# Turning the softmax weights and the inverse sums of a four-layer graph network with the DMA crossbar instead of TensorE

## The chip, the cores and the metric

The kernel runs on one core of a Trainium2 chip. The metric is the device time of one execution in microseconds (us), median of several.

## The reference, cut to what matters

Four graph-attention layers, each behind a layer norm and a relu, each added to its input. There are 32 independent items of 512 nodes with 256 features, all in float32.

```python
h = relu(layernorm(x)); x = x + L0(h)   # e = leaky(h1 @ h2.T), masked; softmax; relu(att @ h3)
h = relu(layernorm(x)); x = x + L1(h)   # 4 heads: e = leaky(e_src[i] + e_dst[j]), masked; softmax; elu(att @ q)
h = relu(layernorm(x)); x = x + L2(h)   # 4 heads of 64: softmax(Q K^T / 8, masked) @ V, @ Wo + bo, layernorm
h = relu(layernorm(x)); x = x + L3(h)   # 4 heads, as layer 1
```

Layer 0 has one 512 x 512 matrix of softmax weights for each item, layer 2 has four (one for each head). Both come out with the query node on the partitions, and the product with the values wants the key node there. So each must be transposed. Layers 1 and 3 build their weights in the transposed order to begin with.

## The kernel before, in words

An item's activations are tiles of 128 partitions by 512 or 1024 columns. A matrix of weights is four row tiles of 128 x 512. Five engines run programs written out by hand, in order. The program is a software pipeline over the items: `slots` calls `slot(a, b, c, d)` once for each step n, where `a` is item n, `b` item n-1 and so on. In one slot item `a` passes layer 0 and the start of layer 1, item `b` the rest of layer 1 and the start of layer 2, and item `c` the rest of layer 2 and layer 3. The order of the calls in `slot` on each engine is a table found ahead of time; a call waits on semaphores for its inputs, and everything behind it on that engine waits with it. `BANK` says which of the eight PSUM banks a result goes to.

The names that matter: `exp0`/`exp2` (ACT) write the weights of layer 0 into `pA` and of layer 2, head h, into `pA`, `pB`, `pX0`, `pX1`. `weights_transposed0`/`weights_transposed2` (PE, L1017 and L1115) turn a row tile with four 128 x 128 transposes into PSUM, and `weights_out0`/`weights_out2` copy it to SBUF (ACT L486, L573; DVE L696, L806). `aggregate0` (L1029) and `aggregate2` (L1142) are the products with the values. The inverse sums of layer 2 are spread over a tile by `inverse_columns` (ACT), turned by `inverse_spread` (PE, L1126) and copied by `inverse_out` (ACT, L588). An item thus has 4 + 16 + 2 = 22 turned tiles, 88 transposes. `gat_weights` (DVE, L753) builds the weights of layers 1 and 3; `gat_aggregate` (L1080) uses them; `spread` (SP) sends a row vector to DRAM and reads it back broadcast over the partitions, and waits in between. `deviation` (POOL, L364 and L367) computes the inverse deviation of a norm. `idle_turns` (L966) are matmuls without use where the pipeline is not full.

Of the kernel before, what the change touches and what calls it, by code (L numbers as in the profile page):

```python
# [5 lines left out]
def gnn_stack_kernel(nc, x, adj, W1, W2, W3, gat1_W, gat1_a, Wq, bq, Wk, bk, Wv, bv, Wo, bo,  # L6
# [6 lines left out]
    i32 = mybir.dt.int32  # L13
    ALU = mybir.AluOpType
# [3 lines left out]
    P = 128  # L18
# [8 lines left out]
    SETS = 3  # L27
    ROUNDS = (B - 2) // SETS
# [7 lines left out]
    with ctx:  # L36
# [25 lines left out]
        x_in = sets("x_in", [P, NT, C])  # L62
# [75 lines left out]
        class Work:  # L138


            def __init__(self, c, i=None):
                self.c, self.i, self.s = c, i, c % SETS

            def count(self, per, k):
                return self.c * per + k if self.i is None else self.i * (SETS * per) + (self.c * per + k)

            def turn(self, per, k):

                t = self.c // SETS
                return t * per + k if self.i is None else self.i * per + (t * per + k)  # L150
# [105 lines left out]
        x2_ready = Signal("x2_ready")  # L256

# [28 lines left out]
        def slots(eng, first, slot):  # L286

            first(Work(0))
            for n in range(1, B + 2):
                slot(*[Work(n - d) if 0 <= n - d < B else None for d in range(SETS + 1)])  # L290
# [5 lines left out]
        def _(sp):  # L296
            def load(w, ahead=SETS):
                s, n = w.s, w.count(1, ahead)
                if w.i is not None:
                    n = sp.snap(n)  # L300
                sp.dma_start(x_in[s][:, :, :], x_dram[n]).then_inc(x_loaded[s], 16)

            def store(w):
# [3 lines left out]
                if w.i is not None:  # L307
                    n = sp.snap(n)
# [999 lines left out]
```

## Time and profile before

| | before |
|---|---|
| median of 3 runs | 2943.65 us (2943.62 to 2944.19) |
| span of the profiled execution | 2943.7 us |
| busy: PE, DVE, ACT, POOL | 98%, 72%, 57%, 28% |
| steps of the pipeline | first, then 33 slots |
| share of the DMA engines' time, all hardware queues | 10.8% |

The profiled execution stands at its median, so the span is worked with as it is. The busy share of PE is near one for the whole span; the rows further down show a slot at a time.

### The profile page before, as it was taken

The numbers are of one execution on the slowest core, as the hardware profiler recorded it, in microseconds if no ns is written. First come the engines' busy times: TensorE is split into PE (matmuls) and PEld (weight loads), VectorE is DVE, ScalarE is ACT, GpSimd is POOL, SyncE is SP. The second block draws the span as 40 slices with busy tenths as digits, with TensorE's granted clock in tenths as the row PEclk, the third lists the DMA queues.
The fourth block names the chain that finished last, engine by engine and source line by source line (L and its number), as shares of the span: only waits on it lengthen the run. The fifth ranks groups of instructions, "written<-read, shape, count | busy, mean of one in ns | idle before, by whom it ended". The sixth has DMA issues, their size and how long they took to land.

```text
span 2943.7 us, 68275 instructions
## 1 busy us (share of the span) xinstructions
PE 2887.3 (98%) x27732; PEld 2034.8 (69%) x27732; DVE 2127.5 (72%) x5596; ACT 1682.3 (57%) x3554; POOL 827.8 (28%) x917
## 2 busy tenths in 40 slices
PE   7899999999999999999999999999999999999998
PEld 5566767666767666767667767667767667776766
DVE  5576787776787776877776877776877777877764
ACT  2555655655656655656655656656656656656543
POOL 2123222323222323222233232233222233222221
PEclk9999999999999999999999999999999999999999
DMA  3001011101011101011101011101011111011010
GB/s 102 22 23 45 27 41 45 44 23 45 23 44 45 44 23 44 23 44 44 38 30 44 23 45 44 37 30 44 23 45 44 34 33 40 28 37 37 17 36 30
DMA packets 58840, 109.89 MB, mean 37 GB/s; under 512 B 5568, under 2 KB 41408, under 8 KB 58528
## 3 DMA queue, kind: packets, MB, share of 16 engines
q1 hardware_dynamic: 58032, 104.61, 10.8%
q8 instruction: 220, 3.60, 0.5%
q0 software_dynamic: 496, 0.92, 0.3%
q14 instruction: 92, 0.75, 0.1%
HBM read 88.21 MB, written 17.30 MB: 36 GB/s over the span
## 4 chain that ended last, share of the span: by engine, by line
PE 77%; DVE 12%; POOL 6%; issue 2%; ACT 1%; SPq 0%; DMA 0%; POOLq 0%; DVEq 0%; ACTq 0%
PE ps L972 19%; PE ps L1080 11%; PE ps L1106 8%; PE ps L1115 8%; PE ps L978 8%; PE ps L1142 8%; PE ps L1029 8%; PE ps L958 4%; DVE stats L641 3%; POOL rstd L367 3%; POOL xc L417 3%; DVE pB L753 2%; PE ps L1017 2%; DVE nb L658 1%; DVE hn L829 1%
## 5 line engine op out<-in xcount | busy, mean ns | idle before, releaser
L389 POOL TENSOR_TENSOR qx<-qx,xc 128x512 f32<-128x512 f32 x128 | 163.7, 1279 | 869.4 <-ACT qx L529 869.4
L641 DVE BATCH_NORM_STATS2 stats<-xc 128x6 f32<-128x256 f32 x384 | 134.7, 413 | 328.6 <-POOL xc L399 264.1
L448 ACT ACTIVATE hn<-xc,nb,rstd 128x256 f32<-128x256 f32 x384 | 209.1, 592 | 163.9 <-DVE nb L658 160.7
L1080 PEld LDWEIGHTS ps<-vals,pA 128*64 128x64 f32 x8192 | 253.9, 138 | 54.6 <-issue 54.5
L972 PE MATMUL ps<-wgat,hT 128*128 128x264 f32 x1024 | 267.4, 395 | 1.8 <-ACT hT L457 1.8
L1080 PE MATMUL ps<-vals,pA 128*64 128x65 f32 x8192 | 266.4, 223 | 2.1 <-DVE pA L753 2.0
L1080 PE MATMUL ps<-vals,pB 128*64 128x65 f32 x8192 | 264.0, 223 | 0.3 <-DVE pB L753 0.2
L1080 PEld LDWEIGHTS ps<-vals,pB 128*64 128x64 f32 x8192 | 249.7, 138 | 16.8 <-issue 16.7
L457 ACT COPY hT<-ps 128x1024 f32<-128x1024 f32 x128 | 129.7, 1013 | 224.0 <-PE ps L958 219.8
L1106 PE MATMUL ps<-qx,qT 64*128 64x512 f32 x1024 | 249.8, 614 | 1.1 <-DVE hn L767 0.8
L364 POOL TENSOR_SCALAR rstd<-mv 128x4 f32<-128x4 f32 x160 | 75.0, 469 | 610.2 <-DVE mv L650 610.2
L1029 PE MATMUL ps<-vals,pB 128*128 128x256 f32 x1024 | 243.2, 381 | 1.1 <-ACT vals L469 1.1
L1142 PE MATMUL ps<-pX,vals 128*64 128x512 f32 x512 | 233.6, 599 | 2.3 <-DVE pA L806 2.3
L978 PE MATMUL ps<-hT,wqkvo 128*128 128x512 f32 x512 | 233.0, 598 | 0.8 <-ACT hT L457 0.8
L1008 PE MATMUL ps<-hT,qT 128*128 128x512 f32 x512 | 228.3, 599 | 1.1 <-ACT qT L463 1.1
L1029 PEld LDWEIGHTS ps<-vals,pB 128*128 128x128 f32 x1024 | 190.6, 191 | 38.9 <-issue 14.8
L972 PEld LDWEIGHTS ps<-wgat,hT 128*128 128x128 f32 x1024 | 179.5, 190 | 50.4 <-issue 24.9
L958 PE MATMUL ps<-ident,hn 128*128 128x128 f32 x1024 | 199.0, 280 | 11.9 <-ACT hn L448 11.1
L958 PEld LDWEIGHTS ps<-ident,hn 128*128 128x128 f32 x1024 | 132.3, 141 | 105.3 <-DVE rowmax L667 32.7
L367 POOL TENSOR_TENSOR rstd<-rstd,minus_half 128x4 f32<-128x4 f32 x160 | 192.5, 1203 | 13.3
L753 DVE SCALAR_TENSOR_TENSOR pA<-qT,gval,adjT 128x512 f32<-128x512 f32 x248 | 184.5, 785 | 6.7 <-DMA hT<-r_dram 6.5
L562 ACT ACTIVATE pX<-pX,negmax 128x512 f32<-128x512 f32 x256 | 183.4, 720 | 0.6 <-DVE negmax L797 0.6
(147 smaller groups left out, 6194.3 us busy)
## 6 DMA issues: line engine op xcount, KB each, us to landing
qT<-r_dram SPq DMA_DIRECT2D x64, 512.0 KB, 3.9
hT<-r_dram SPq DMA_DIRECT2D x64, 512.0 KB, 4.9
x_in<-in_x SPq DMA_DIRECT2D x32, 512.0 KB, 3.9
out_x<-xc SPq DMA_DIRECT2D x32, 512.0 KB, 3.0
pX<-in_adj SPq DMA_DIRECT2D x1, 1024.0 KB, 8.1
r_dram<-growT SPq DMA_DIRECT2D x64, 8.0 KB, 1.3
pX<-in_L_gnn_W SPq DMA_DIRECT2D x2, 256.0 KB, 5.2
pA<-in_L_gnn_a POOLq DMA_DIRECT2D x8, 64.0 KB, 8.8
```

The source lines that it names most:

```text
L367: nc.gpsimd.tensor_tensor(rstd[s][:, :], rstd[s][:, :], minus_half[:, :], ALU.pow).then_inc(rstd_ready[norm].sem, 1)
L641: last = nc.vector.bn_stats(stats[s][:, t, :], src[:, t, :])
L753: last = nc.vector.scalar_tensor_tensor(out=gat_p[s][h % 2][:, t, :], in0=row, scalar=gval[s][:, 1, t, h:h + 1], in1=adjT[:, t, :], op0=AL ...
L958: last = nc.tensor.transpose(ps[:, bank + k, t * P:(t + 1) * P], hn[s][:, t, k * P:(k + 1) * P], ident[:, :])
L972: last = nc.tensor.matmul(at, src[w.s][:, k, t * P:(t + 1) * P], wt[:, k, 0:width], start=(k == 0), stop=(k == KT - 1))
L978: last = nc.tensor.matmul(ps[:, bank + m, :], wt[:, k, m * P:(m + 1) * P], hT[w.s][:, k, :], start=(k == 0), stop=(k == KT - 1))
L1008: last = nc.tensor.matmul(ps[:, BANK[f"E{t}"], :], qT[s][:, k, t * P:(t + 1) * P], hT[s][:, k, :], start=(k == 0), stop=(k == KT - 1))
L1029: last = nc.tensor.matmul(rows_in(BANK["A"])[:, t, :], pB[s][:, t, j * P:(j + 1) * P], vals[s][:, j, 0:C], start=(j == 0), stop=(j == NT - 1))
L1080: last = nc.tensor.matmul(ps[lo:hi, BANK[f"G{g}.{h}"], t * DV:(t + 1) * DV], gat_p[s][h % 2][:, j, t * P + lo:t * P + hi], vals[s][:, j, h ...
L1106: last = nc.tensor.matmul(ps[:, BANK[f"S{p}.{t}"] + hh, :], qT[s][at, p, t * P:(t + 1) * P], kT[s][at, p, :], start=True, stop=True)
L1115: last = nc.tensor.transpose(ps[:, BANK[f"PT{h}.{t}"], j * P:(j + 1) * P], prob2[w.s][h][:, t, j * P:(j + 1) * P], ident[:, :])
L1142: last = nc.tensor.matmul(ps[hh * D:(hh + 1) * D, BANK[f"G2.{p}"], :], vals[s][:, j, h * D:(h + 1) * D], probT2[s][h][:, :, j * P:(j + 1) ...
```

## The change

Every one of the 22 tiles is turned by the DMA crossbar, which transposes 16-bit elements. A float32 tile of 128 x 512 is handled as two 16-bit halves of each word. First a **split** on POOL or DVE writes the tile as 128 x 2 x 512 (all low halves, then all high halves) into one of three ring buffers `halves`. Then SP issues a DMA transpose of 128 x 8 x 128 16-bit elements (the **turn**), back into the tile that the weights came from. Then a **join** on ACT or DVE interleaves the halves again into the destination (`pB`, `probT2`, or `qT` for the inverse sums). A split waits until the turn three places earlier in `TURNS` has landed.

In a slot 19 of the splits are POOL's and 3 DVE's; 14 of the joins are ACT's and 8 DVE's. The 88 transposes, the 12 copies on ACT and the 10 on DVE are gone. The order of all engines and the `BANK` table are new. `slot` now takes `(z, a, b, c, d, e)`: the norm of item n+1 (`z`) is started a slot early, and the last three aggregations of layer 3 and its end move into the next slot (`d`), so there are 34 slots. Input tiles are two instead of three. The two places where PE spread the row vector of a lone item (`BY_PE`) and the `idle_turns` within slots are gone.

```diff
+        halves = [sb(f"halves{r}", [P, 2, N], u16) for r in range(RING)]
...
+        TURNS = (
+            (2, (2, 3, 0)), (2, (2, 2, 1)), (2, (2, 3, 1)), (2, (2, 2, 2)), (2, (2, 3, 2)),
...
+        def turn(sp, w, tile):
+            sp.dma_start_transpose(words(w, tile).rearrange("p (b n) -> p b n", n=P),
+                                   turns.half(w, tile)[:, :, :].rearrange("p q n -> p (q n)")).then_inc(
+                                       turns.sem_of(w, tile), 16)
...
+            def turn2(w, h, t):
+                if w is None:
+                    return
+                line = split_by_pool if (w.c, (2, h, t)) in split_by_pool.at else split_by_dve
+                line.wait(sp, w, (2, h, t))
+                turn(sp, w, (2, h, t))
...
+            def split2(w, h, t):
+                if w is None:
+                    return
+                p2_ready[h].wait(pool, w, t + 1)
+                turns.landed(pool, w, (2, h, t), 1)
+                nc.gpsimd.tensor_copy(turns.half(w, (2, h, t))[:, :, :], pairs(w, (2, h, t))).then_inc(split_by_pool.sem, 1)
...
-            def weights_out2(w, h, t):
-                if w is None:
-                    return
-
-
-                if h == 3 and t == 1:
-                    agg2_ready.wait(act, w, 1)
-                pT2p_ready[h].wait(act, w, t + 1)
-                nc.scalar.copy(probT2[w.s][h][:, t, :], ps[:, BANK[f"PT{h}.{t}"], :]).then_inc(pT2_act[h].sem, 1)
...
+            def join2(w, h, t):
+                if w is None:
+                    return
+                turns.landed(act, w, (2, h, t))
+                nc.scalar.copy(joined(w, (2, h, t)), flat(w, (2, h, t))).then_inc(pT2_act[h].sem, 1)
...
-            def weights_transposed2(w, h, t):
-                if w is None:
-                    return
-                p2_ready[h].wait(pe, w, t + 1)
-                for j in range(NT):
-                    last = nc.tensor.transpose(ps[:, BANK[f"PT{h}.{t}"], j * P:(j + 1) * P],
-                                               prob2[w.s][h][:, t, j * P:(j + 1) * P], ident[:, :])
-                last.then_inc(pT2p_ready[h].sem, 1)
```

The orders at three places. First TensorE, from one `aggregate2` to the next in the slot where item 1 is `c` (the last digit of a name is its buffer set). Before:

```order
L1142 MATMUL ps<-pX2,vals1 64x512
L1142 MATMUL ps<-pA1,vals1 64x512
L1115 MATMUL ps<-ident,pX1 128x128 x4
L1115 MATMUL ps<-ident,pX0 128x128 x8
L1115 MATMUL ps<-ident,pX1 128x128 x12
L1126 MATMUL ps<-ident,qx1 128x128 x8
L1142 MATMUL ps<-pB1,vals1 64x512
L1142 MATMUL ps<-pX2,vals1 64x512
```

And in the changed kernel, at the same place:

```order
L1212 MATMUL ps<-pX2,vals1 64x512
L1212 MATMUL ps<-pA1,vals1 64x512
L1172 MATMUL ps<-vals2,pA2 64x65 x32
L1067 MATMUL ps<-ident,hn0 128x128 x8
L1172 MATMUL ps<-vals2,pB2 64x65 x32
L1087 MATMUL ps<-hT0,wA 128x512 x4
L1172 MATMUL ps<-vals2,pA2 64x65 x32
L1172 MATMUL ps<-vals2,pB2 64x65 x32
L1212 MATMUL ps<-pB1,vals1 64x512
```

The transposes of weights and inverse sums are gone, and layer 1's aggregations of item 2 stand between the two.

Second POOL, around the norm of layer 2's output (`mv_ready_in`) and the norm of layer 3 (`mv_ready_3`) of item `c`. Before:

```order
L364 TENSOR_SCALAR rstd2<-mv2 128x4 [waits mv_ready_in]
L367 TENSOR_TENSOR rstd2<-rstd2,minus_half 128x4 [waits var_eps_in]
L417 TENSOR_TENSOR xc2<-xc2,hn2 128x1024 [waits og_ready,xb_ready]
L389 TENSOR_TENSOR qx0<-qx0,xc0 128x4x128 [waits elu_r_1]
L364 TENSOR_SCALAR rstd2<-mv2 128x4 [waits mv_ready_3]
```

After:

```order
L511 COPY halves1<-pA0 128x1024 [waits turned1,p0_ready]
L450 TENSOR_SCALAR rstd1<-mv1 128x4 [waits mv_ready_in]
L453 TENSOR_TENSOR rstd1<-rstd1,minus_half 128x4 [waits rstd_ready_in]
L511 COPY halves2<-pA0 128x1024 [waits turned2,p0_ready]
L493 TENSOR_TENSOR xc2<-xc2,b_rows 128x1024 [waits hn_ready_2]
L503 TENSOR_TENSOR xc1<-xc1,hn1 128x1024 [waits og_ready,xb_ready]
L511 COPY halves0<-pA0 128x1024 [waits turned0,p0_ready]
L450 TENSOR_SCALAR rstd1<-mv1 128x4 [waits mv_ready_3]
```

Splits (COPY) of layer 0's weights now stand ahead of both deviations.

Third SP's queue, around the row vector of layer 3. Before:

```order
L322 DMA r_dram3_0<-growT0 16x128 [waits rT_out_3]
L326 DMA qT0<-r_dram3_0 128x1024 [waits r_written_3]
L326 DMA hT0<-r_dram3_0 128x1024
L301 DMA x_in2<-in_x 128x4x256 [waits x1_ready]
L322 DMA r_dram1_2<-growT2 16x128 [waits rT_out_1]
```

After:

```order
L316 DMA_TRANSPOSE pA1<-halves0 128x8x128 [waits split_by_pool]
L316 DMA_TRANSPOSE pA1<-halves1 128x8x128 [waits split_by_pool]
L384 DMA r_dram3_0<-growT0 16x128 [waits rT_out_3]
L388 DMA qT0<-r_dram3_0 128x1024 [waits r_written_3]
L388 DMA hT0<-r_dram3_0 128x1024
L316 DMA_TRANSPOSE pB1<-halves2 128x8x128 [waits split_by_dve]
L316 DMA_TRANSPOSE pB1<-halves0 128x8x128 [waits split_by_pool]
```

All 22 turns of a slot go through this one queue, in between the same spreads.

## Rows read from the trace of the kernel before

**Rows 1.** The page, part 1: busy time and share of each engine
```profile
PE 2887.3 (98%) x27732; PEld 2034.8 (69%) x27732; DVE 2127.5 (72%) x5596; ACT 1682.3 (57%) x3554; POOL 827.8 (28%) x917
```

**Rows 2.** A window of one slot: length, busy time by engine, clock, DMA
```profile
1378.60:1467.20 88.60, 88.23 (x860) 61.92 (x856) 65.95 (x174) 52.42 (x112) 25.65 (x28) 1.00 0.11 37
```

**Rows 3.** Timeline of PE: aggregate2 starting the first and last regular slots
```profile
226.63 0.59 PE L1142 MATMUL ps<-pX,vals 128*64 128x512 f32 x1
...
2796.33 0.59 PE L1142 MATMUL ps<-pX,vals 128*64 128x512 f32 x1
```

**Rows 4.** The chain that ended last, within one slot: start, us, what
```profile
1382.11 2.77 PE ps L1115 x24
...
1410.15 1.58 POOL rstd L367
...
1417.62 0.44 PE ps L1017 x4
```

**Rows 5.** Timeline, copies of turned tiles in a row: start, us
```profile
1472.28 0.69 DVE L806 COPY pB<-ps 128x512 f32<-128x512 f32 x1
1472.88 1.28 DVE L806 COPY pX<-ps 128x512 f32<-128x512 f32 x2
1473.77 0.59 ACT L573 COPY pX<-ps 128x512 f32<-128x512 f32 x1
1474.25 1.08 ACT L588 COPY qx<-ps 128x512 f32<-128x512 f32 x2
```

**Rows 6.** Groups by form: busy us, mean ns of one, idle before
```profile
L876 DVE TENSOR_SCALAR pX<-pX 128x2048 f32<-128x2048 int32 x1 | 1.2, 1217 | 0.0
L871 DVE COPY pX<-ps 128x1024 f32<-128x1024 f32 x1 | 1.2, 1225 | 1.2 <-PE ps L1230 1.2
L580 ACT COPY qx<-rinv 128x512 f32<-128x512 f32 x64 | 39.2, 612 | 0.0
L457 ACT COPY hT<-ps 128x1024 f32<-128x1024 f32 x128 | 129.7, 1013 | 224.0 <-PE ps L958 219.8
L417 POOL TENSOR_TENSOR xc<-xc,hn 128x1024 f32<-128x1024 f32 x32 | 75.7, 2364 | 128.2 <-DVE hn L837 128.2
L364 POOL TENSOR_SCALAR rstd<-mv 128x4 f32<-128x4 f32 x160 | 75.0, 469 | 610.2 <-DVE mv L650 610.2
L367 POOL TENSOR_TENSOR rstd<-rstd,minus_half 128x4 f32<-128x4 f32 x160 | 192.5, 1203 | 13.3
L837 DVE TENSOR_TENSOR hn<-hn,b_rows 128x1024 f32<-128x1024 f32 x32 | 38.9, 1214 | 2.2 <-ACT hn L448 2.2
```

**Rows 7.** Timeline of DVE and POOL where their instructions meet
```profile
1438.47 1.12 DVE L753 SCALAR_TENSOR_TENSOR pA<-qT,gval,adjT 128x512 f32<-128x512 f32 x1
1437.26 1.78 POOL L377 TENSOR_TENSOR vals<-qx,gval 128x256 f32<-128x256 f32 x3
1439.01 0.67 POOL L364 TENSOR_SCALAR rstd<-mv 128x4 f32<-128x4 f32 x1
```

**Rows 8.** Timeline of DVE and POOL, elsewhere
```profile
1409.84 0.23 POOL L364 TENSOR_SCALAR rstd<-mv 128x4 f32<-128x4 f32 x1 [1.29 <-DVE mv L650]
1474.37 2.70 DVE L753 SCALAR_TENSOR_TENSOR pA<-qT,gval,adjT 128x512 f32<-128x512 f32 x4
1475.26 1.39 POOL L367 TENSOR_TENSOR rstd<-rstd,minus_half 128x4 f32<-128x4 f32 x1
1451.95 0.74 DVE L753 SCALAR_TENSOR_TENSOR pB<-qT,gval,adjT 128x512 f32<-128x512 f32 x1
```

**Rows 9.** DMA queues and issues: size, median us from issue to landing
```profile
q1 hardware_dynamic: 58032, 104.61, 10.8%
...
qT<-r_dram SPq DMA_DIRECT2D x64, 512.0 KB, 3.9
hT<-r_dram SPq DMA_DIRECT2D x64, 512.0 KB, 4.9
...
r_dram<-growT SPq DMA_DIRECT2D x64, 8.0 KB, 1.3
```

**Rows 10.** Waits in one slot: us in all, times, longest
```profile
DVE stats L641 <- POOL xc L399: 8.5, 1, 8.5
```

More of the change, by code:

```diff
@@ L256, in gnn_stack_kernel, with in_order, __init__, wait @@
         x2_ready = Signal("x2_ready")
+        TURNS = (
[4 rows of a table added]
+        )
+        SPLIT_BY_POOL = (
[4 rows of a table added]
+        )
+        SPLIT_BY_DVE = (
+            (0, (0, 0)), (1, (2, 1, 0)), (1, (2, 0, 3)),
+        )
+        def in_order(plan, first):
+            steps = list(first)
+            steps += [(n - stage, tile) for n in range(1, B + LAST) for stage, tile in plan
+                      if 0 <= n - stage < B]
+            return {step: i for i, step in enumerate(steps)}
+        class Splits:
+            def __init__(self, name, plan, first):
+                self.sem, self.at = sem(name), in_order(plan, first)
+            def wait(self, eng, w, tile):
+                if w is not None:
+                    eng.wait_ge(self.sem, self.at[w.c, tile] + 1)
@@ new lines, in gnn_stack_kernel, with __init__, half, sem_of @@
+        class Turns:
+            def __init__(self, name, plan, first):
+                self.sems, self.at = [sem(f"{name}{r}") for r in range(RING)], in_order(plan, first)
+            def half(self, w, tile):
+                return halves[self.at[w.c, tile] % RING]
+            def sem_of(self, w, tile):
+                return self.sems[self.at[w.c, tile] % RING]
+            def landed(self, eng, w, tile, before=0):
+                if w is None:
+                    return
+                i = self.at[w.c, tile]
+                if i // RING + 1 - before > 0:
+                    eng.wait_ge(self.sems[i % RING], 16 * (i // RING + 1 - before))
@@ L284, in rows_in, with slots @@
             return ps[:, bank:bank + 2, :].rearrange("p b (t c) -> p (b t) c", c=C)
[L286 to L290, printed above, removed]
+        def slots(first, slot):
+            first(Work(0), Work(1))
+            for n in range(1, B + LAST):
+                slot(*[Work(n - d) if 0 <= n - d < B else None for d in range(-1, 5)])
         block = ctx.enter_context(nc.Block())
@@ L296, in _, with load @@
         def _(sp):
[L297 to L301, printed above, removed]
+            def load(w, ahead=X_SETS):
+                sp.dma_start(x_in[w.x][:, :, :], x_dram[w.c + ahead]).then_inc(x_loaded[w.x], 16)
             def store(w):
@@ L341, in _ @@
                 sp.sem_inc(x_stored[s], 16)
-                if s > 0:
+                if 0 < s < X_SETS:
                     load(Work(s), 0)
-            for n in range(B + 2):
-                slot(*[Work(n - d) if 0 <= n - d < B else None for d in range(SETS)], more=n + SETS < B)
+            slots(first, slot)
             for s in range(SETS):
@@ L621, in first @@
+                gat_row_exp(a, 1); gat_exp(a, 1)
                 act.wait_ge(bias_in, BIASES)
                 act.wait_ge(setup_ok, SETUP)
-            slots(act, first, slot)
+            slots(first, slot)
         @block.vector
@@ L647, in mean_and_variance @@
                 s = w.s
[L648 removed]
+                mv_ready[norm].wait_apart(dve, w, 1)
                 for t in range(NT):
@@ L656, in shift_of_norm @@
                 s = w.s
-                rstd_ready[norm].wait(dve, w)
+                rstd_ready[norm].wait(dve, w, 2)
                 nc.vector.scalar_tensor_tensor(
@@ new lines, in split0, with split2 @@
+            def split0(w, t):
+                if w is None:
+                    return
+                p0_ready.wait(dve, w, t + 1)
+                turns.landed(dve, w, (0, t), 1)
+                nc.vector.tensor_copy(turns.half(w, (0, t))[:, :, :], pairs(w, (0, t))).then_inc(split_by_dve.sem, 1)
+            def split2(w, h, t):
+                if w is None:
+                    return
+                p2_ready[h].wait(dve, w, t + 1)
+                turns.landed(dve, w, (2, h, t), 1)
+                nc.vector.tensor_copy(turns.half(w, (2, h, t))[:, :, :], pairs(w, (2, h, t))).then_inc(split_by_dve.sem, 1)
```

441 lines of the change are left out of this document (196 added, 245 removed), and 20 rows, old and new, of tables (BANK, SPLIT_BY_POOL, TURNS).

## The prediction

> **What bounds the kernel now.** I read the page's busy shares first. TensorE is busy 98% of the span and the next engine, DVE, 72% [rows 1]. The windows of single slots then show that this is so in every regular slot: of 88.60 us PE works 88.2, DVE 65.9, ACT 52.4 and POOL 25.7, at a granted clock of 1.00 [rows 2]. The reader is to see two things there: PE leaves 0.4 us, and DVE leaves 22.7 us, of which a good part is waiting with nothing to do (8.5 us for the residual of layer 0 alone [rows 10]). So the time of a slot is PE's own work, and what is taken off PE comes off the slot until another engine, or the path through one item, holds it.
>
> How many slots this holds for I take from the start of `aggregate2`, which opens a slot: the first regular one starts at 226.63 us and the last full one ends at 2796.33, 29 slots of 88.61 us [rows 3]. The ends of the pipeline are the rest, 226.6 + 147.4 = 374.0 us. The span, 2943.7, is also the median of the runs, so nothing is to be scaled.
>
> **What the change takes off PE.** 88 transposes a slot: 16 of layer 0, 64 of layer 2, 8 of the inverse sums. The chain of waits gives their pace where they are the path: 24 in 2.77 us and 4 in 0.44 [rows 4], 0.110 to 0.115 each. I take 0.110: 88 x 0.110 = 9.7 us. The products stay, in other order and other banks. The new floor of a slot on PE is 88.6 - 9.7 = 78.9 us.
>
> **What it does to ACT.** Twelve copies go. One lasts 0.59 us, and the next starts 0.48 after it (two last 1.08), so a pace of 0.49 [rows 5]: -5.9 us. Fourteen joins of 1024 16-bit elements come. No row shows one; the nearest are a 512-element copy from SBUF at 0.61 us and a 1024-element copy from PSUM at 1.01 [rows 6]. Near the second, as the elements count: 0.95 in a row, +13.3 us (bounds +7 and +14). ACT comes to 59.8 us of 78.9. It has room.
>
> **What it does to DVE.** Ten copies go: 0.69 us each, the next one starting 0.60 later [rows 5], at 0.61 each -6.1. Eight joins and three splits come. From PSUM 1024 elements take 1.22 us; but an operation with one SBUF input does 2048 elements in 1.22 [rows 6], so 1024 in 0.62. The joins read and write SBUF, so I take the second: 11 x 0.62 = +6.8; bound above 11 x 1.22 = +13.4. DVE comes to 66.7 us (73.3 by the bound).
>
> **What it does to POOL.** Nineteen splits come. POOL's nearest row is a two-input operation of 1024 elements at 2.36 us [rows 6]. A split has one input; I take half, 1.2 us, with 2.36 as the upper and 0.6 as the lower bound (twice the pace again, for 16-bit elements). 19 x 1.2 = 22.8; POOL comes to 48.5 us (37 to 70.5). Still no bound by itself.
>
> **What DVE and POOL do to each other.** This is the price that the busy shares hide. A `gat_weights` (two SBUF inputs) takes 0.74 us alone [rows 8]. The one at 1438.47 takes 1.12, and POOL's group that began at 1437.26 ends at 1439.04: it was held for 0.38 us. The POOL instruction of 0.67 at 1439.01 takes 0.23 elsewhere, and ends its wait with that `gat_weights` [rows 7, 8]. So the two hold each other up. Not always: four `gat_weights` in 2.70 us run at full pace beside a POOL instruction of four columns [rows 8]; what holds is the wide operation. The Trainium skill has this rule in "SBUF — State Buffer", section "SBUF: two separate sides": DVE, when it has two SBUF inputs or runs in a two-port mode, and GpSimd share a pair of ports as an exclusive lock for the whole instruction. The row at 1438.47 agrees.
>
> How much it can be: POOL's wide work is now 25.7 less five deviations of 0.47 + 1.20 [rows 6] = 17.3 us, and 17.3 + 22.8 = 40.1 after. DVE's instructions with two SBUF inputs are 32 `gat_weights`, 4 `lrelu0` and 4 `gat_out` at a pace of 0.67 (2.70 for four) and one `times_gamma` at 1.21: 28.0; with the 11 splits and joins 34.8. Laid at random into 78.9 us they meet for 40.1 x 34.8 / 78.9 = 17.7 us, of which each side waits about half. DVE would be at 66.7 + 8.8 = 75.5 of 78.9: close, but under the floor.
>
> **What lies on the path through an item.** DVE's waits were slack while PE had 88 us of work; now the path matters. In the last part of a slot item `c` goes from layer 2's output through two norms to the row vector of layer 3, and item `a` through the norm of layer 1. Each passes a `deviation` on POOL (1.05 to 1.58 us in the chain [rows 4]), and the new order puts a split just ahead of each. Three of them behind a split of 1.2 us each: 3.6 us. Add two collisions of the size seen, 0.38 to 0.44: 0.9. So I take 4.5 us of PE's waiting in a slot: 83.4 us. DVE waits 8.5 us for `residual0`'s sums now [rows 10], and that slack takes the rest. Queued behind a waiting deviation are the next splits, and for them waits SP.
>
> **What the turns cost.** No row shows a DMA transpose. The bounds are 1.3 us (8 KB) and 4.9 us (512 KB broadcast) from issue to landing [rows 9]; a turn moves 262 KB, and I take about 3. With three ring buffers, 1.2 + 3 us divided by three is 1.4 us a turn, 22 turns are 31 us of 78.9. The traffic goes from 104.6 MB at 10.8% to 289 MB, at that pace 30%. So hidden, but for its place in the path of layer 0 (split, turn, join about 5 us, where a transpose and a copy took about 1); the starting of the next item's norm a slot early gives that back. "Advanced Engine Details and Errata", section "X-Bar Transpose (TRN2)", of the Trainium skill gives 350 to 400 GB/s: an estimate of 0.7 us for a turn's data, by which the sum stays the same.
>
> **The ends.** 374 us before. About three items' transposes fall in them, but there the path counts and PE's work doesn't. Against it stand exposed turns (some 5 us in each of about three places) and two round trips through DRAM of 1.3 + 4.9 us that PE made before. I leave the ends at 374.
>
> **The sum.** 29 x 83.4 + 374 = 2418.6 + 374 = 2792.6, so 2793 us, 5.1% less.
>
> **The rivals.** (1) *PE stays the bound.* The order was found with the collisions in it, and PE waits for 0 to 1 us in a slot. For it: the order before leaves PE 0.4 us. 29 x 79.5 + 374 = 2680. Chance 0.12. (2) *The shared ports and the path take it all back.* One mechanism: nearly all POOL's wide work meets DVE's, and DVE pays. It decides from 88.6 - 4.5 - 66.7 = 17.4 us of waiting on DVE in a slot, just the whole random overlap. For it: the splits stand in POOL where DVE has 24 `gat_weights` on end. With the splits at 2.36 us POOL's wide work is 62.1, the overlap 27.4, a slot 66.7 + 27.4 = 94.1 at least, the time 3103; at 1.2 us with all overlap on DVE 88.9, the time 2952. Against it: DVE's non-SBUF work (over 30 us) is free for POOL. Chance 0.17, and a quarter of it is still faster. (3) *The crossbar or SP takes one turn after another.* It decides at 88.6 / 22 = 4.0 us a turn. At 4.9 each, with the two DRAM writes of 1.3 that SP waits for, a slot is 110.4 us and the time 3576. For it: nothing in the trace excludes it, all 22 stand in one queue. Against it: two 512 KB reads issued together land at 3.9 and 4.9, so they overlap. Chance 0.16. That the transposes are not really gone is excluded by the order of PE.
>
> **How the numbers follow.** Forecast 0.55 (slots of 80.5 to 86.5 us: 2709 to 2883), rival 1 0.12, rival 2 0.17, rival 3 0.16. Within 0.2%, 6 us, is what a measurement can't tell from no change. Faster: 0.55 + 0.12 + 0.04 = 0.71; same 0.03; slower 0.26. The range leaves out rival 3 and the upper end of rival 2, 0.20 together: from the floor without a wait, 29 x 78.9 + 374 = 2662, to slots of 90.9, 3010.
>
> **What would show it.** Regular slots near 83.4 us; PE busy near 78.5 in each and waiting for joined weights or for `hn` behind a deviation; DVE at 73 to 77 busy, with `gat_weights` of 1 us and more beside POOL's COPY; POOL near 50; a split at 1.2 and a DVE join at 0.62; turns landing in about 3 us. Wrong if turns come every 4 us or more (SP or the crossbar full), if a split takes over 2 us, or if PE waits for under 1 us or over 8 us in a slot.

## The result, and the profile after

The changed kernel takes 3236.1 us (median of 4 runs, 3231.1 to 3242.2), the kernel before 2943.9 us beside it: ratio 1.099, 95% interval 1.098 to 1.101. The forecast was 2793 us and faster; the range, to 3010, misses it too. It came out on the side of rival 2, and beyond the 3103 us of its upper end. Two executions further down (one each of c1 and e1) had a much lower granted clock, 0.76 and 0.58, and are left out of the medians.

The page of the changed kernel, part 1, then the granted clock of its slices, for [rows 1]:

```profile
PE 2696.3 (83%) x24604; PEld 1797.0 (56%) x24604; DVE 2638.4 (82%) x5628; ACT 2028.3 (63%) x3618; POOL 1703.4 (53%) x1525
...
PEclk8898999999999999999999999999999999999987
```

Two slots in the middle and the mean of three, for [rows 2]:

```profile
1425.90:1522.80 96.90, 83.39 (x778) 56.15 (x774) 80.92 (x176) 63.47 (x114) 51.07 (x46) 0.93 0.47 89
1522.80:1619.80 97.00, 81.25 (x772) 54.06 (x769) 82.59 (x176) 63.21 (x114) 52.32 (x48) 0.96 0.47 96
...
sum 291.10, PE 247.20 PEld 165.39 DVE 245.58 ACT 189.52 POOL 157.09; mean PE 82.40 PEld 55.13 DVE 81.86 ACT 63.17 POOL 52.37
```

TensorE did lose work: 88.3 us of a slot became 82.4, and with it 3128 instructions. But the slot grew. From the second `aggregate2` start at 262.6 us to the one 29 slots later at 3064.6 a slot is 96.62 us, against 88.61 [rows 3]; and the ends are 3233.0 - 2802.0 = 431.0 us against 374.0. Of the 289 us between the spans 232 are slots and 57 are ends. No engine is full: VectorE (DVE) has 82 of 97, TensorE (PE) 82. What TensorE waited for in the second slot of the window above (us in all, times, longest):

```profile
PE ps L1146 <- DVE dm L809: 6.7, 2, 6.5
PE ps L1172 <- DVE pB L849: 6.5, 3, 2.9
```

`dm` is a small reduction on VectorE (`gat_max_t`, 128 x 4), the first step of layer 1's softmax shift; L849 is `gat_weights`. For `hn` behind a deviation, on which the prediction had put its waiting, TensorE waited four times in the whole run (20.3 us), each time outside the regular slots.

The groups by form say what grew (busy us, mean ns of one | idle before), for [rows 5, 6]. The four `gat_weights` groups (L849) took 741 to 785 ns in the same view of before, 737 us in all with the two small groups that read their row from PSUM:

```profile
L518 POOL COPY halves<-pX 128x1024 uint16<-128x1024 uint16 x256 | 344.2, 1363 | 343.9 <-DMA pB<-halves 199.3 <-DMA pX<-halves 139.0 <-ACT pX L667 5.4
...
L849 DVE SCALAR_TENSOR_TENSOR pA<-qT,gval,adjT 128x512 f32<-128x512 f32 x256 | 299.9, 1212 | 15.1 <-DMA hT<-r_dram 14.8
L849 DVE SCALAR_TENSOR_TENSOR pB<-qT,gval,adjT 128x512 f32<-128x512 f32 x256 | 299.6, 1219 | 0.0
...
L849 DVE SCALAR_TENSOR_TENSOR pA<-hT,gval,adjT 128x512 f32<-128x512 f32 x256 | 241.1, 989 | 2.5 <-PE ps L1172 2.5
L849 DVE SCALAR_TENSOR_TENSOR pB<-hT,gval,adjT 128x512 f32<-128x512 f32 x256 | 236.9, 986 | 5.1 <-PE ps L1172 4.8
...
L689 ACT COPY pA<-pB 128x1024 uint16<-128x1024 uint16 x96 | 128.7, 1340 | 2.1 <-DMA pB<-halves 2.1
...
L947 DVE COPY pB<-pA 128x1024 uint16<-128x1024 uint16 x64 | 108.8, 1755 | 5.3 <-DMA pA<-halves 5.3
```

`gat_weights` take 1077.5 us now, 340 more; that is 11 of VectorE's 16 additional us in a slot. The last row is a join of layer 0: 1.76 us on average, where most joins on VectorE take 0.75. The timeline shows why: the two of a slot last 3.53 us together, beside GpSimd's (POOL's) residual of layer 2, which is old work in a new place, and only the end of it beside a split.

```profile
1469.95 3.53 DVE L947 COPY pB<-pA 128x1024 uint16<-128x1024 uint16 x2
1470.18 2.70 POOL L503 TENSOR_TENSOR xc<-xc,hn 128x1024 f32<-128x1024 f32 x1 [1.28 <-DVE hn L925]
```

The turns, for [rows 9] (packets, MB and share of the time of 16 DMA engines; then the us to the landing):

```profile
q1 hardware_dynamic: 801456, 289.25, 45.9%
...
pA<-halves SPq DMA_TRANSPOSE x256, 3.2
pX<-halves SPq DMA_TRANSPOSE x256, 4.0
pB<-halves SPq DMA_TRANSPOSE x128, 5.3
```

One place shows how a slot gets long. Timeline near the end of a slot (start, us, engine, line; in brackets the idle time before it and what ended it). SyncE's rows come first:

```profile
1589.94 0.32 SPq L384 DMA_DIRECT2D r_dram<-growT  x1
1591.67 0.34 SPq L388 DMA_DIRECT2D qT<-r_dram  x1
1592.05 1.29 SPq L388 DMA_DIRECT2D hT<-r_dram  x1
1593.38 4.63 SPq L316 DMA_TRANSPOSE pB<-halves  x2
```

```profile
1587.67 0.68 DVE L941 COPY halves<-pB 128x1024 uint16<-128x1024 uint16 x1
...
1599.24 0.69 DVE L941 COPY halves<-pA 128x1024 uint16<-128x1024 uint16 x1 [3.64 <-DMA pB<-halves]
1599.85 0.74 DVE L953 COPY pA<-pB 128x1024 uint16<-128x1024 uint16 x1
1600.23 1.24 POOL L518 COPY halves<-pX 128x1024 uint16<-128x1024 uint16 x1 [4.66 <-DMA pB<-halves]
1600.48 4.42 DVE L849 SCALAR_TENSOR_TENSOR pA<-qT,gval,adjT 128x512 f32<-128x512 f32 x3
1601.42 1.50 POOL L518 COPY halves<-pB 128x1024 uint16<-128x1024 uint16 x1
1604.82 0.17 DVE L809 TENSOR_REDUCE dm<-qx 128x4 f32<-128x16 f32 x1
1605.04 0.37 PE L1146 MATMUL ps<-ident,dm 128*4 128x128 f32 x1 [6.46 <-DVE dm L809]
```

Tile (2,1,0), layer 2's head 1, row tile 0, was split by 1588.35. Its turn stands behind `spread(c, 3)` in SyncE's order and is issued at 1593.38. VectorE splits (2,0,3) next, into the ring buffer that this turn must free, and waits 3.64 us for it. Then three `gat_weights`, 2.07 us in a row before, last 4.42 beside GpSimd's splits, and only then comes the small `dm`, for which TensorE has idled 6.46 us.

### The profile page after: what moved, and what is told of

Read it like the earlier page. It is cut to its first block and busy times, and to the rows that moved or that the text cites. A ratio compares the mean times of both kernels' runs of the same rounds, so it can differ in the third digit from the quotient of the medians.

```text
span 3233.0 us, 63869 instructions
## 1 busy us (share of the span) xinstructions
PE 2696.3 (83%) x24604; PEld 1797.0 (56%) x24604; DVE 2638.4 (82%) x5628; ACT 2028.3 (63%) x3618; POOL 1703.4 (53%) x1525
## 5 line engine op out<-in xcount | busy, mean ns | idle before, releaser
L518 POOL COPY halves<-pX 128x1024 uint16<-128x1024 uint16 x256 | 344.2, 1363 | 343.9 <-DMA pB<-halves 199.3
L475 POOL TENSOR_TENSOR qx<-qx,xc 128x512 f32<-128x512 f32 x128 | 209.0, 1633 | 311.6 <-ACT qx L634 311.6
L1172 PEld LDWEIGHTS ps<-vals,pA 128*64 128x64 f32 x8192 | 304.5, 161 | 114.5 <-issue 113.9
L1172 PE MATMUL ps<-vals,pA 128*64 128x65 f32 x8192 | 322.1, 248 | 52.9 <-DVE pA L849 52.7
L849 DVE SCALAR_TENSOR_TENSOR pA<-qT,gval,adjT 128x512 f32<-128x512 f32 x256 | 299.9, 1212 | 15.1 <-DMA hT<-r_dram 14.8
L849 DVE SCALAR_TENSOR_TENSOR pB<-qT,gval,adjT 128x512 f32<-128x512 f32 x256 | 299.6, 1219 | 0.0
L463 POOL TENSOR_TENSOR vals<-qx,gval 128x256 f32<-128x256 f32 x256 | 245.7, 979 | 15.1 <-ACT gval L625 15.1
L849 DVE SCALAR_TENSOR_TENSOR pA<-hT,gval,adjT 128x512 f32<-128x512 f32 x256 | 241.1, 989 | 2.5 <-PE ps L1172 2.5
L849 DVE SCALAR_TENSOR_TENSOR pB<-hT,gval,adjT 128x512 f32<-128x512 f32 x256 | 236.9, 986 | 5.1 <-PE ps L1172 4.8
L511 POOL COPY halves<-pA 128x1024 uint16<-128x1024 uint16 x96 | 115.8, 1207 | 207.7 <-ACT pA L590 199.0
```

Of the source, the lines that this page charges most:

```text
L463: last = nc.gpsimd.tensor_tensor(values[:, :, h, 0:D], qx[s][:, :, h * D:(h + 1) * D], gval[s][:, 0, :, h:h + 1].broadcast_to([P, NT, D]), ...
L475: nc.gpsimd.tensor_tensor(elu_a[s][p], elu_a[s][p], xc[s][:, :, p * 2 * D:(p + 1) * 2 * D], ALU.add).then_inc(xr_ready[g].sem, 1)
L518: nc.gpsimd.tensor_copy(turns.half(w, (2, h, t))[:, :, :], pairs(w, (2, h, t))).then_inc(split_by_pool.sem, 1)
L849: last = nc.vector.scalar_tensor_tensor(out=gat_p[s][h % 2][:, t, :], in0=gat_r[s][h], scalar=gval[s][:, 1, t, h:h + 1], in1=adjT[:, t, :] ...
L1172: last = nc.tensor.matmul(ps[lo:hi, BANK[f"G{g}.{h}"], t * DV:(t + 1) * DV], gat_p[s][h % 2][:, j, t * P + lo:t * P + hi], vals[s][:, j, h ...
```

## The experiments

Theory 1: the loss is that GpSimd and VectorE hold each other up on their way to SBUF. Theory 2: it is the turns' latency, the ring of three and SyncE's order. Theory 3: the new order or the joins. The table gives the median of each, the mean slot of 29 (as above) and the busy us of the engines in a slot (mean of three).

| kernel | us | slot | PE | DVE | POOL |
|---|---|---|---|---|---|
| before | 2943.9 | 88.61 | 88.3 | 65.9 | 25.7 |
| after | 3236.1 | 96.62 | 82.4 | 81.9 | 52.4 |
| after, POOL's splits narrow (a1) | 3001.3 | 89.57 | 81.6 | 72.8 | 36.5 |
| after, turns short (a2) | 3218.0 | 96.27 | 83.0 | 82.9 | 56.7 |
| after, both (a3) | 2946.6 | 87.62 | 80.7 | 72.7 | 37.1 |
| after, joins narrow too (a4) | 2894.2 | 86.34 | 81.2 | 67.1 | 35.9 |
| after, ring of four (b1) | 3225.8 | 96.27 | 82.7 | 81.2 | 55.6 |
| after, dm first (e1) | 3237.7 | | | | |
| after, turn ahead of spread (f1) | 3186.6 | 95.13 | 83.0 | 81.7 | 54.0 |
| after, six splits on ACT (c1) | 3266.3 | 97.66 | 83.7 | 74.6 | 44.1 |
| the same, later places (c3) | 3146.4 | 93.91 | 82.1 | 77.4 | 42.5 |
| c3, f1 and e1 together (f2) | 3130.4 | 93.41 | 82.7 | 76.8 | 43.9 |
| before + 19 whole POOL copies (b2) | 3265.8 | 98.98 | 91.6 | 74.9 | 47.3 |
| before + 19 narrow POOL copies (b3) | 2928.7 | 88.08 | 88.1 | 65.4 | 29.7 |
| before + 19 whole, kept behind (b4) | 3087.1 | 93.03 | 89.0 | 72.5 | 49.7 |
| before + 5 narrow (d3) | 2929.4 | 88.07 | 88.0 | 65.4 | 26.7 |
| before, inverse sums by crossbar (d1) | 2979.3 | 89.65 | 87.3 | 66.0 | 25.6 |

### Taking the added work out again

These four leave out a part of the work, to see what it costs. In a1, a3 and a4 GpSimd copies 16 of 1024 half-words in each split; in a2 and a3 a turn moves 128 of 1024 columns and the joins read zeros; in a4 the joins are narrow too. VectorE's three splits a slot stay whole.

```diff
-nc.gpsimd.tensor_copy(turns.half(w, t)[:, :, :], pairs(w, t))
+nc.gpsimd.tensor_copy(turns.half(w, t)[:, :, 0:8], pairs(w, t)[:, :, 0:8])   # a1, a3, a4
-sp.dma_start_transpose(words(...), turns.half(w, tile)...)
+sp.dma_start_transpose(words(...)[:, 0:1, :], turns.half(w, tile)...[:, 0:P])  # a2, a3; a4 to a tile of its own
-nc.scalar.copy(joined(w, t), flat(w, t))
+nc.scalar.copy(joined(w, t)[:, :, 0:8], zeros[:, :, 0:8])                     # a4, and on VectorE
```

> The changed kernel (3236 us) with GpSimd's 19 splits of a slot copying 16 of their 1024 half-words; the rest of the split is left out, the turns and the joins stay whole. Theory 1, GpSimd and VectorE hold each other up (in the profile after, the gat_weights rows take 0.99 and 1.22 us where they took 0.74 to 0.79, about 11 us a slot, and VectorE is busy 82 of 97 us): gat_weights return to 0.75 us, VectorE falls to about 70 us a slot, the slot to 84 to 88 us, 2820 to 2930 us in all. Theory 2, the turns' landing (3.2 to 5.5 us) and the ring of three set the slot: the waits for a turn stay, VectorE's rows may get shorter but the slot stays above 93 us, 3120 us or more. Theory 3, the new order or the joins set it: the same, 3120 us or more.

> The changed kernel with each turn moving 128 of its 1024 columns (32 KB where 262 KB went); the joins read a tile of zeros with the same length instead of what was turned, so the weights are zero; splits and joins keep their size. Theory 1 (GpSimd against VectorE): splits and gat_weights stay as slow as they are, VectorE stays above 80 us a slot, 3130 to 3240 us. Theory 2 (landing and ring): a turn lands in about 2 us, the waits of GpSimd and VectorE on the ring vanish, slot 85 to 89 us, 2850 to 2970 us. Theory 3 (order, joins): 3130 us or more.

> Both at once: narrow splits on GpSimd and short turns, joins whole (zeros). Theory 1: little under the run with narrow splits alone (within 30 us of it). Theory 2: little under the run with short turns alone. If both costs carry weight, lower than either by 50 us or more; if only the order or the joins matter, still 3100 us or more.

> Everything that was added made small: GpSimd's splits and all joins at 16 half-words, turns of 128 columns, VectorE's three splits whole. What is left is the new order and PSUM table on the old work, less 88 transposes. If the order is as good as before, TensorE's 78 us or so of work sets the slot and it takes 2620 to 2720 us. Theory 3 (the order itself costs): 2800 us or more.

Narrow splits gave back 235 us (ratio to before 1.019, 1.018 to 1.021), short turns alone 18 (1.093, 1.092 to 1.095). The first is above the 2820 to 2930 us that I gave theory 1 and below the 3120 of the others. So GpSimd's splits carry most of the loss, and the turns' data and landing hardly any while the splits are whole. Two things limit this. Narrow splits also shorten GpSimd's own row by 16 us a slot, so what stands behind them comes sooner; this run doesn't tell that from shared access. And `gat_weights` are still 804 us in all, not 737, and the join of layer 0 is as long as it was, so it isn't the splits that hold it:

```profile
L949 DVE COPY pB<-pA 128x1024 uint16<-128x1024 uint16 x64 | 108.9, 1755 | 5.3 <-DMA pA<-halves 5.3
```

With narrow splits in place, short turns gave 55 us more, and narrow joins another 52. What surprised me is the last kernel: all additions small, 88 transposes gone, and still 2894 us (0.983, 0.981 to 0.984), not 2620 to 2720. Its waits in one slot (engine, line, us in all, times, longest):

```profile
PE ps L1154 <- DVE dm L814: 1.9, 2, 1.7
PE ps L1160 <- DVE dmax L821: 1.1, 2, 0.7
PE ps L1180 <- DVE pB L854: 0.8, 2, 0.6
```

The rows are of one slot and come to 4.1 us with the smallest waits. In the mean TensorE is idle for about 5 us of 86.3 and works 81, not 78.5. In the run with narrow splits and short turns (a3), one slot has the clock at 0.98 and its neighbour at 1.00:

```profile
1561.80:1649.80 88.00, 81.40 (x771) 53.75 (x768) 73.47 (x176) 63.10 (x114) 37.50 (x50) 0.98 0.15 45
1649.80:1735.00 85.20, 79.55 (x775) 52.71 (x773) 71.86 (x175) 62.90 (x114) 36.38 (x44) 1.00 0.17 46
```

At the full clock the same work takes 79.55, near the forecast's 78.5. The rest is a part of the time at the lower of TensorE's two levels (1.2 against 2.4 GHz); the slots that I read of before are all at 1.00, and in them TensorE idles 0.3 to 0.4 us, not 5 to 7. So theory 3 may have a share: 88 transposes less, at 0.110 us each, would be 280 us in 29 slots, and 50 came. The other 230 are the new order, what is left of the additions, the clock and the ends (391 us against 374), not told apart.

### The costs by themselves

A kernel of stages, each with 8 to 24 of one instruction on one engine, alone or beside another's, run once. It has nothing of the network. The pace is a stage's length divided by its count; the mean is that of one instruction, and is longer than the pace where the next begins before the last has ended.

> Only the disputed instructions, stage after stage, alone and in pairs; it leaves out the whole network. Theory 1 (GpSimd and VectorE take turns at a shared way to SBUF): the gat_weights form (512 columns, two SBUF inputs) takes 0.74 us alone and 1.2 to 1.6 us beside GpSimd's splits, the splits 1.05 us alone and 1.5 us or more beside it; beside turns or ScalarE's joins alone it stays at 0.74 to 0.80. Rival (the SBUF is slowed by the transfers of the turns): the row beside turns shows 0.9 us or more and the row beside the splits stays near 0.75. The masked maximum out of PSUM beside splits: in between, 0.65 to 0.9. ScalarE's join 1.34 us alone, unchanged beside the splits. A turn alone lands in about 3 us, three under way in 3 to 5 us each.

Groups within single stages: `gat_weights`' form alone; splits alone; both together (two rows); the form beside turns; the masked maximum (PSUM and SBUF inputs) and the splits beside each other (two rows); VectorE's join beside splits:

```profile
L42 DVE SCALAR_TENSOR_TENSOR weights<-row,col,adjT 128x512 f32<-128x512 f32 x16 | 10.7, 744 | 0.1
...
L62 POOL COPY halves_p<-pair_src 128x1024 uint16<-128x1024 uint16 x16 | 15.8, 1040 | 12.8 <-SPq L118 12.8
...
L42 DVE SCALAR_TENSOR_TENSOR weights<-row,col,adjT 128x512 f32<-128x512 f32 x16 | 23.1, 1517 | 36.8 <-SPq L118 36.8
L62 POOL COPY halves_p<-pair_src 128x1024 uint16<-128x1024 uint16 x16 | 22.7, 1466 | 20.7 <-SPq L118 20.7
...
L42 DVE SCALAR_TENSOR_TENSOR weights<-row,col,adjT 128x512 f32<-128x512 f32 x24 | 16.0, 748 | 3.3 <-SPq L118 3.3
...
L62 POOL COPY halves_p<-pair_src 128x1024 uint16<-128x1024 uint16 x16 | 15.8, 1040 | 58.8 <-SPq L118 58.8
L46 DVE CUSTOM_DVE_ANT_0 masked<-ps,adjT 128x512 f32<-128x512 f32 x24 | 14.7, 685 | 0.1
...
L51 DVE COPY joined_v<-flat_src 128x1024 uint16<-128x1024 uint16 x17 | 24.5, 1536 | 0.1
```

Alone the form comes every 0.67 us and a split every 0.99; together one of each every 1.42. Their starts alternate strictly, one of each: VectorE's row doubles, GpSimd's grows by 0.43. The join does the same though it has one input. The masked maximum, with one input in PSUM, is not touched. Turns leave the `gat_weights` form (0.748 against 0.744) and ScalarE's join (1.32) as they are, and a split doesn't touch ScalarE's join either; splits beside turns had no stage. The Trainium skill states the rule in "SBUF — State Buffer", section "SBUF: two separate sides": an exclusive lock for the whole instruction, against VectorE with two SBUF inputs or in a two-port mode. This case's rows agree as to the alternation, with the 1.517 and 1.536 above. They don't as to the whole: a pair comes every 1.42 us, and 0.67 + 0.99 would be 1.66, so 0.24 of it still overlaps. Whether the join runs in a two-port mode no run here shows. A turn alone lands in 3.1 to 3.6 us, and its issue holds SyncE for 1.23 to 1.36 us.

### The shared access, without a crossbar

```diff
+    def added(count): ... nc.gpsimd.tensor_copy(spare[:, :, 0:WIDE], pairs of adjT[:, :, 0:WIDE])
-    gat_values(b, 1); deviation(a, 0); deviation(c, "in"); residual2(c); ...
+    gat_values(b, 1); added(3); deviation(a, 0); added(3); deviation(c, "in"); added(1); residual2(c); ...  # b2: 512, b3: 8
+    deviation(a, 0); nb_ready[0].wait(pool, a); added(8); ... deviation(a, 1); nb_ready[1].wait(pool, a); added(11)  # b4
```

> The kernel before with 19 more GpSimd copies a slot, each of the split's form (1024 half-words out of pairs) from a constant tile to a spare one; nothing waits for their data and no turn is made. Theory 1: gat_weights lengthen from 0.75 to about 1.0 to 1.1 us, VectorE goes from 66 to about 77 us of a slot, and since the TensorE work is still 88 us the slot grows to 91 to 97 us: 3030 to 3170 us. Rival (the loss comes from the turns, the ring and the new order): VectorE keeps 66 us and the time stays within 1% of 2944 us.

> The control of the run before it: the same 19 GpSimd copies at the same places with 16 of 1024 half-words each. What it takes over 2944 us is the delay of GpSimd's other work behind the inserted instructions, at some 0.5 us each. Both theories: 2940 to 2990 us; if it is as slow as the full copies, the delay of what stands behind them is the cost, and not shared access.

> The kernel before with 19 whole copies a slot on GpSimd (as in the run that took 3266 us), but in the two stretches in which GpSimd idles 11 and 24 us and only after nb has been written, so that no deviation and no nb stands behind them. What is left is that VectorE's wide instructions share access with them. If VectorE's length is what counts: VectorE 66 to about 74 us of a slot and 3030 us or more. If it is the short chain deviation, nb, hn that made the other run slow, and VectorE's 22 us of room take the rest: 2944 to 2990 us.

Nineteen whole copies a slot, on which nothing depends, cost the kernel before 322 us (1.109, 1.108 to 1.111): more than the whole change, and more than I gave theory 1. The narrow ones cost nothing; they gain 15 us. But the 322 are several things. The granted clock fell from 0.997 to 0.977. And with a copy right behind each of the five deviations, and ahead of three of them, the `nb` after it (the shift of the norm, 128 x 4 elements on VectorE) went from 359 to 967 ns, and ScalarE's waits for it from 417.5 us in all to 718.3. The group, and the row of the waits:

```profile
L673 DVE SCALAR_TENSOR_TENSOR nb<-mv,rstd 128x4 f32<-128x4 f32 x160 | 154.7, 967 | 147.8 <-POOL rstd L368 146.9
```

```profile
ACT hn L463 <- DVE nb L673: 718.3, 160, 18.0
```

Kept behind `nb`, in stretches where GpSimd idles, the same 19 copies cost 143 us (1.048, 1.047 to 1.050):

```profile
1535.00:1628.00 93.00, 89.04 (x860) 61.80 (x858) 72.49 (x174) 52.48 (x112) 49.66 (x47) 1.00 0.11 36
```

VectorE works 6.6 us more, and the slot is 4.4 longer, though VectorE has 20 us of room in it. Room elsewhere doesn't cover:

```profile
1546.28 10.80 POOL L428 COPY spare<-adjT 128x1024 uint16<-128x1024 uint16 x8 [1.83 <-DVE nb L671]
1550.67 4.40 DVE L766 SCALAR_TENSOR_TENSOR pA<-hT,gval,adjT 128x512 f32<-128x512 f32 x3
1555.00 1.21 DVE L842 TENSOR_TENSOR hn<-ps,b_rows 128x1024 f32<-128x1024 f32 x1
1556.26 1.98 PE L991 MATMUL ps<-hT,wA 128*128 128x512 f32 x4 [1.77 <-DVE hn L842]
```

Three `gat_weights` last 4.40 where they lasted 2.07. TensorE doesn't wait for them here, but for layer 2's bias addition (L842) behind them on VectorE: 1.77 us, the largest of its waits in this slot. My expectation of 3030 or more was right, but its "VectorE's length is what counts" isn't what the row shows; 72.5 of 93 is no bound.

### The turns, the ring and SyncE's order

```diff
-    RING = 3
+    RING = 4                                                       # b1; growT one each for layers 1 and 3, not three
-    softmax_shift2(b, 1); split2(b, 0, 3); join2(b, 1, 0); ... gat_max_t(a, 1)
+    softmax_shift2(b, 1); gat_max_t(a, 1); split2(b, 0, 3); join2(b, 1, 0)   # e1
-    turn2(b, 0, 1); spread(c, 3); turn2(b, 1, 0)
+    turn2(b, 0, 1); turn2(b, 1, 0); spread(c, 3)                   # f1
```

> The changed kernel with four buffers of halves instead of three (the row buffers of layer 1 and 3 are one each instead of three, to make room). In the changed kernel GpSimd waits 199, 139 and 68 us in all for a turn that frees the ring, and VectorE 97 us at its split of (2,0,3), behind which dm is late and TensorE waits 6.5 us a slot. If the ring sets the path (theory 2): VectorE's wait at that split goes, TensorE's wait for dm falls by about 3 us, 3110 to 3180 us. If only the shared access counts (theory 1): the splits come closer together and run beside the same VectorE work, 3215 to 3250 us.

> The changed kernel with VectorE's gat_max_t(a, 1) ahead of its split (2,0,3), and gat_max and gat_shift ahead by a step; the same instructions, another order. If TensorE's 6.5 us wait for dm is a part of the path by itself: it shrinks to about 3 us (qx is ready at 1598.4, dm came at 1604.8), the slot falls by 3 to 4 us, 3110 to 3150 us. If VectorE's own length bounds the slot (82 of 97 us, stretched by GpSimd), the wait moves to gat_aggregate(c, 3, 0) and the time stays at 3220 to 3250 us.

> The changed kernel with SyncE's turn of (2,1,0) ahead of spread(c, 3) instead of behind it. With a fourth buffer VectorE's wait at its split (97 us in all) only moved to its next join (86 us) for the same turn, so not the ring is late there but that turn, in SyncE's order. If VectorE's own row of work and waits sets the slot (82 us of work and 15 of waits in 97): the wait of 3.0 us a slot goes and the time falls by 60 to 100 us, to 3135 to 3175 us. If the wait is cover for something else: within 15 us of 3236.

The fourth buffer (for which the row buffers of layers 1 and 3 went from three to one each) gave 10 us (1.095, 1.094 to 1.097). VectorE's wait at the split went and came back one instruction later, at the join of the same late turn:

```profile
DVE pA L953 <- DMA pB<-halves: 86.0, 31, 4.6
```

Dm first gave nothing (1.099, 1.097 to 1.101); no rows stand here for it, so where its wait went is not shown. The turn ahead of `spread` gave 50 us (1.082, 1.080 to 1.084), not the 60 to 100 I expected: TensorE's waits for dm fell from 180 to 108 us, but VectorE waits 87 us for the rows of layer 3 instead, which `spread` now brings later:

```profile
DVE pA L849 <- DMA hT<-r_dram: 86.8, 47, 6.9
```

### Splits on ScalarE

```diff
-    exp2(c, 3, 3); join2(c, 0, 3); exp2(c, 2, 2); ...; v_out(c, 2); elu_relu(d, 3, 0); ...
+    exp2(c, 3, 3); split2(c, 2, 1); join2(c, 0, 3); ...; split2(c, 3, 2); v_out(c, 2); ...           # c1
+    exp2(c, 3, 3); join2(c, 0, 3); ...; v_out(c, 2); split2(c, 2, 1); elu_relu(d, 3, 0); ...          # c3
```

> The changed kernel with the six splits that GpSimd makes around gat_values(b, 1), of heads 2 and 3, made by ScalarE instead (six times 1.34 us, ScalarE goes from 63 to 71 us of a slot); all of the work is done. Theory 1: the gat_weights of layer 1 at the slot's start fall from 1.2 to about 0.8 us, VectorE loses some 4 to 6 us a slot, and the slot goes from 97 to 92 to 94 us: 3070 to 3150 us. Theory 2 (landing and ring set the slot): no gain, 3200 us or more, as the turns are as many and ScalarE waits for them in its order.

> The six splits on ScalarE again, but behind v_out(c, 2) and spread over the work behind it, since in the first version TensorE waited 172 us in all for vals of v_out. All of the work is done. If the 7 us a slot that VectorE got back in the first version (82 to 75 us) are worth something on the path (theory 1), the time falls to 3080 to 3170 us. If VectorE's length isn't what bounds the slot, it stays at 3210 us or more.

> Six splits on ScalarE (later places), the turn of (2,1,0) ahead of spread(c, 3), and dm first, together. If what each gives adds up: 90 us of the six splits and 60 to 100 us of the turn, 3040 to 3090 us, VectorE about 77 us of a slot of 91 to 93. If GpSimd's and VectorE's shared access only moves with it: 3120 us or more. In no case under 2944 us, as with all splits of GpSimd narrow it was 3001.

The first version was slower than the changed kernel (1.111, 1.107 to 1.114), where I had expected 3070 to 3150 us, though VectorE had 7 us less: I had put ScalarE's splits ahead of `v_out`, and TensorE waited for it.

```profile
PE ps L1222 <- ACT vals L582: 172.1, 31, 11.2
```

Behind `v_out` the same six gave 90 us (1.068, 1.067 to 1.070). A split takes ScalarE 1.04 us. Together with the turn and dm it was 3130 us (1.063, 1.061 to 1.065), where the sum of the single gains would be 3097. That is above the 3040 to 3090 for gains that add up, in the 3120 or more that I had put on a shared access that only moves, and still 6% slower than before.

### What can be had from the kernel before

```diff
+    # five times a slot, behind each deviation: one copy of 16 half-words               (d3)
-    inverse_spread: four transposes each; nc.scalar.copy(kT[w.s][:, p, :], ps[...])
+    sp.dma_start_transpose(qT rows, kT rows as halves); nc.scalar.copy(joined kT, flat qT)   # d1
```

> The kernel before with one GpSimd copy of 16 half-words behind each of the five deviations of a slot; its result is used by nothing. With 19 of them the kernel took 2929 us, and the row of nb (128x4) fell from 359 to 161 ns: by the theory of shared access, GpSimd's next wide instruction no longer begins in the moment in which VectorE wants to write nb. If so, five are enough: nb at about 161 ns, 2925 to 2932 us. If the gain came from elsewhere (the other 14, their places), 2940 us or more.

> The kernel before with only the two tiles of inverse sums turned by the crossbar: ScalarE writes their halves itself (two copies of 512 instead of one), SyncE turns them, ScalarE joins both after both have landed; no split on GpSimd or VectorE, eight transposes a slot less on TensorE (0.9 us). All of the work is done. If a turn's way (some 3.3 us, and 1.3 us of SyncE for each) is hidden behind aggregate2: 2915 to 2930 us. If norm2 and what follows wait for it: 2950 to 3050 us.

Five narrow copies: 2929.4 us, 0.9946 of before (0.9931 to 0.9961), the same as with nineteen. It does all of the work and is half a per cent faster than the kernel before. Its `nb`:

```profile
L671 DVE SCALAR_TENSOR_TENSOR nb<-mv,rstd 128x4 f32<-128x4 f32 x160 | 25.6, 160 | 57.3 <-POOL rstd L368 56.4
```

359 ns became 160, and the slot 88.61 became 88.07. The 359 were an average: in the kernel before, 130 of 160 take under 0.2 us and 30 some 1.2, the latter beside a wide `gat_residual` (L389) that GpSimd starts at the same moment. In d3 none does. The two inverse tiles by crossbar, with no split on GpSimd at all, cost 1.2% (1.010 to 1.013): TensorE works 1.0 us less and the slot is 1.0 longer. Most of that is a wait of 1.6 us a slot, which the kernel before doesn't have: `aggregate2` comes right behind the last transposes of weights and waits for ScalarE's copy of them; in the kernel before, the eight transposes of inverse sums stand between the two. `norm2` on VectorE now waits for the join too, of which TensorE feels 0.4 us.

```profile
PE ps L1154 <- ACT pX L581: 50.5, 32, 1.6
DVE qT L834 <- ACT qx L599: 66.5, 33, 4.8
```

## Why the prediction was wrong

**Right.** What is left of TensorE's work: 79.55 us at the full clock (a3), where 78.5 was forecast. POOL's split alone 0.99 to 1.04 us (I took 1.2), VectorE's join 0.63 in a row (0.62), a turn about 3 us alone. That the crossbar isn't the bound: rival 3 is out, as short turns give 18 us. Traffic grew to 289 MB as worked out, but at 46% of the DMA engines' time and not 30%. ScalarE's joins last 1.34 us, every 1.20, and not 0.95: ScalarE is at 63.2 and not 59.8, with room to spare.

**The step that failed** is in "What DVE and POOL do to each other": "Laid at random into 78.9 us they meet for ... 17.7 us, of which each side waits about half. DVE would be at ... 75.5 of 78.9: close, but under the floor." Two things in it were wrong. The size: VectorE works 81.9 us, 15.2 above my 66.7 and not 8.8. Of the 15.2, 9.1 go when GpSimd's splits are narrow, and 2.0 are the two joins of layer 0, which the new order put beside a residual that GpSimd had to make before as well. The costs by themselves show how it comes: beside a stream of splits VectorE's instruction goes from 0.74 to 1.52, and the splits stand where `gat_weights` come 24 in a row. I had written that against myself under rival 2 and still took a random layout. And "under the floor" was no test, which is the worse error: in the kernel before, 6.6 us more of VectorE's work lengthened the slot by 4.4 with 20 us of room left. What is held, or stands behind what is held on VectorE, is what TensorE waits for at that moment. With the splits narrow, 9.1 us of VectorE's time and 7.1 of the slot come back together.

**The term of the sum** in which this shows is TensorE's waiting, in "So I take 4.5 us of PE's waiting in a slot: 83.4 us." A slot has 14.2, beyond the 8 that I had named as a sign of being wrong, and not for my reason: for `hn` behind a deviation TensorE doesn't wait in any regular slot. It waits 6.5 us for `gat_weights` and 6.7 for dm, behind a late turn and held `gat_weights`, which I had not looked for.

**Mis-sized beside it.** I costed turns at "hidden", with 1.4 us each from ring and landing, and did not ask what else stands in SyncE's queue: `spread`, with its trip through DRAM of some 3.4 us, holds one turn a slot, and that turn ahead of it gave 50 us. The ends: I left them at 374 us and they are 431; with narrow splits 403, with all small 391, so about half of the 57 go with whole splits. TensorE's clock: I took 1.00, and the three slots in the middle show 0.93 to 0.96, some 2 to 3 us of its 82.4, in slots in which it isn't the bound.

**Rival 2** was the mechanism, in part. Its decision point, 17.4 us more on DVE, wasn't reached (15.2 by the busy time), and the slot grew all the same, because that point too took VectorE's whole room as cover. It gave 2952 for all overlap on DVE at 1.2 us a split: a slot of 84.4 us of VectorE and 4.5 of waiting, 88.9. (Its upper slot, 94.1, leaves those 4.5 out.) Measured are 81.9 of VectorE and 14.7 in which it stands still; the 284 us that 2952 lacks are 224 of slots and 57 of ends. Experiments put prices on parts of it that overlap and don't add up: the turn behind `spread` 50 us, the joins 52. With every addition small the order still makes 2894 and not 2793. How much of that last 101 us is the order and how much the narrow instructions that still stand in it (each narrow split waits for its turn too) was not told apart. Nor was GpSimd's own length apart from shared access in the changed kernel; shared access alone has a price only in the kernel before, 143 us for the same 19 copies.

## What to carry to other kernels

Before moving work to GpSimd, list what VectorE does at that very place, and what stands behind it there. Beside instructions with SBUF inputs only, the two engines' wide instructions nearly add up (1.42 us a pair, 0.67 and 0.99 alone), and unused time of VectorE elsewhere doesn't pay for it; the cheapest test is to put idle copies of that form into the kernel as it is. A transfer in place of an engine's work is to be costed with what stands ahead of it in its queue, and with what waits in order behind whoever waits for it. And a floor found by taking work off the bound engine is only a floor: here an order with all additions small gave back a fifth of what the arithmetic offered.

## What the hardware did that I had not expected

A 16-bit copy with one SBUF input is held as fully as a three-operand instruction (0.73 to 1.54 us beside GpSimd's split), while VectorE's 512-column maximum with one input in PSUM (0.69) is not. A 128 x 4 instruction on VectorE takes 160 ns, but 1.2 us where a wide GpSimd instruction begins with it (1411.76 beside 1411.70 in the kernel before); one idle GpSimd copy of 16 half-words in between is worth 0.5% of the kernel. The issue of a DMA transpose held SyncE for 1.23 to 1.36 us, a plain transfer's for 0.3 to 1.3.
